# DLRM tower on one core: pairs of 8, 16, 24, six of 32 and 16 samples, layer 2 of two pairs in waits, unread products on TensorE

## The reference, cut to what matters

```python
x0 = e                       # (512, 32, 16), e[:, m] = tbl_m[ids[:, m]]
xk, outs = x0, []
for W in (W0, W1, W2):       # (32, 32, 64), (32, 64, 64), (32, 64, 64)
    xk = relu(einsum('bmd,bhd,mhk->bkd', x0, xk, W))
    outs.append(sum(xk, axis=2))
h = concatenate([concatenate(outs, 1), dense_ctx], 1)      # 512 x 208
h = maximum(h @ W_top1 + b_top1, 0)
h = maximum(h @ W_top2 + b_top2, 0)
y = h @ W_top3
```

## Time and profile before

| | |
|---|---|
| median of 3 runs | 350.59 us |
| profiled execution, its own time | 353.74 us |
| its span, first to last instruction | 351.9 us |
| TensorE matmul busy | 305.4 us (87%) |
| VectorE busy | 274.2 us (78%) |
| GpSimd busy | 254.2 us (72%) |
| ScalarE busy | 61.6 us (18%) |
| mean granted TensorE clock | 0.985 |

### The profile page before, as it was taken

The page is one execution under the profiler, slowest core; times in us unless marked ns, Lnnn a source line. Parts: engine busy times, 40 slices in busy tenths (PEclk is TensorE's granted clock), DMA queues, the critical chain, the costliest instruction groups (busy, mean ns, idle before and its releaser), DMA issues. The chain is left out here.

```text
span 351.9 us, 3914 instructions
## 1 busy us (share of the span) xinstructions
PE 305.4 (87%) x1476; PEld 112.7 (32%) x1476; DVE 274.2 (78%) x173; ACT 61.6 (18%) x122; POOL 254.2 (72%) x193
## 2 busy tenths in 40 slices
PE   0016859798999988999999999999999999998986
PEld 0013513243334222323333333233333334333426
DVE  0024949799999969999999999999999788954201
ACT  1001210301220330012201220222031104113011
POOL 5775678879788988888898879898919567917000
PEclk9999996999999999999999999999999999999998
DMA  5374956957973984286338643952580102100000
GB/s 178 45 251 83 369 111 180 376 88 213 381 149 65 279 329 80 28 337 260 56 71 303 272 72 77 378 190 61 151 327 0 45 2 63 45 2 0 0 0 0
DMA packets 52282, 52.07 MB, mean 148 GB/s; under 512 B 37574, under 2 KB 42568, under 8 KB 49064
## 3 DMA queue, kind: packets, MB, share of 16 engines
q1 hardware_dynamic: 41272, 39.92, 34.2%
q10 hardware_dynamic: 6896, 10.85, 11.5%
q0 software_dynamic: 4096, 1.06, 3.0%
HBM read 41.33 MB, written 2.10 MB: 123 GB/s over the span
## 5 line engine op out<-in xcount | busy, mean ns | idle before, releaser
L519 DVE TENSOR_TENSOR z_vector<-left,r_forms 128x2048 f32<-128x2048 f32 (+3 forms) x140 | 260.0, 1924 | 45.4 <-DMA r_forms<-x_rows 23.0
L569 PE MATMUL result<-z_vector,w_sb 128*64 128x512 f32 (+2 forms) x1056 | 213.9, 557 | 41.5 <-DVE z_vector L519 40.2
L309 POOL DMA_INDIRECT gathered_rows<-table,row_index x128 | 121.8, 951 | 41.2 <-issue 34.5
L324 POOL TENSOR_TENSOR z_pool<-r_forms,xj_forms 128x1024 f32<-128x1024 f32 (+2 forms) x60 | 131.8, 2232 | 24.7 <-PE result L569 15.0
L569 PEld LDWEIGHTS result<-z_vector,w_sb 128*64 128x64 f32 x1056 | 77.3, 142 | 172.9 <-issue 143.4
L569 PE MATMUL result<-z_pool,w_sb 128*64 128x512 f32 (+2 forms) x240 | 51.8, 571 | 0.0
L384 ACT ACTIVATE x_sb<-result 128x512 f32<-128x512 f32 (+2 forms) x27 | 14.9, 551 | 169.7 <-PE result L569 169.7
L499 DVE TENSOR_REDUCE d_sums<-x_sb 128x32 f32<-128x512 f32 (+2 forms) x27 | 16.8, 625 | 20.0 <-ACT x_sb L384 20.0
L569 PEld LDWEIGHTS result<-z_pool,w_sb 128*64 128x64 f32 x240 | 15.7, 136 | 34.1 <-issue 33.2
L368 ACT ACTIVATE left<-xj_forms 128x512 f32<-128x512 f32 (+2 forms) x36 | 18.6, 547 | 17.1 <-DMA xj_forms<-x_sb 6.8
L359 ACT ACTIVATE left<-h_form 128x512 f32<-128x512 f32 (+2 forms) x18 | 10.0, 553 | 59.8 <-DVE z_vector L519 44.9
(11 more groups left out here) (32 smaller groups left out, 28.1 us busy)
## 6 DMA issues: line engine op xcount, KB each, us to landing
r_forms<-x_rows SPq DMA_DIRECT2D x24, 1024.0 KB, 10.4
r_forms<-x_rows SPq DMA_DIRECT2D x8, 768.0 KB, 6.8
xj_forms<-x_sb ACTq DMA_DIRECT2D x24, 256.0 KB, 4.0
h_form<-x_rows SPq DMA_DIRECT2D x12, 256.0 KB, 3.0
gathered_rows<-table,row_index POOLq DMA_INDIRECT x128, 3.3
r_forms<-x_rows SPq DMA_DIRECT2D x4, 512.0 KB, 6.1
x_rows<-gathered_rows SPq DMA_DIRECT2D x24, 64.0 KB, 2.5
xj_forms<-x_sb ACTq DMA_DIRECT2D x8, 192.0 KB, 3.1
```

Of the source, the lines that this page charges most:

```text
L309: nc.gpsimd.indirect_dma_start(gathered_rows[:, half % GATHERED, g], None, table, bass.IndirectOffsetOnAxis(ap=row_index[:, at:at + 1], ax ...
L324: nc.gpsimd.tensor_tensor(z_pool[:, unit % NZP, t, :, 0:columns(p)], r_form(q, p, t)[:, s0:s1], xj1_forms[form_buffer(n, p)][:, t, 0:colum ...
L519: nc.vector.tensor_tensor(z_vector[:, unit % NV, t, 0:s1 - s0, 0:columns(p)], left[:, t, bank, 0:columns(p)].unsqueeze(1).broadcast_to([12 ...
L569: done = nc.tensor.matmul(result[n][K * t:K * t + K, 0:columns(p)], weights, z[:, t, 0:columns(p)], start=first, stop=last)
```

## The change

`SAMPLES` becomes 8, 16, 24, six of 32 and 16, so there are ten pairs in place of nine, and the first and the last are smaller. The start of the program is in another order: layer 2 of pairs 0 and 1 moves forward, between the stages of layers 0 and 1 of the next pairs, and (2, 1) is done in two parts (its units 0 and 1 before (1, 2), the others behind (0, 3)). POOL has no chunks in (1, 0), (2, 0), (1, 1) and (2, 1), 2 in (1, 2), and in the last pairs the numbers that the last pairs had before. POOL issues 12 gathers at once and 28 in fours behind waits, and then, as before, 8 behind its products of each stage in which it has chunks. TensorE gets `busy`, unread products of 256 columns, 5 and 2 and 4 and 4 of them in its waits at the start, and 3 ahead of the last part of the tower.

```diff
-SAMPLES = [16, 24] + [32] * 6 + [24]
+SAMPLES = [8, 16, 24] + [32] * 6 + [16]
...
+SPLIT = 1
+STAGES = [(0, 0, "all"), (1, 0, "all"), (0, 1, "all"), (2, 0, "all"), (1, 1, "all"), (0, 2, "all"), (2, 1, "form 0"),
+          (1, 2, "all"), (0, 3, "all"), (2, 1, "form 1")]
+for _p in range(SPLIT + 2, NP):
+    STAGES.append((1, _p, "all"))
     if _p + 1 < NP:
-        STAGES.append((0, _p + 1))
-    if _p > 0:
-        STAGES.append((2, _p - 1))
+        STAGES.append((0, _p + 1, "all"))
+    STAGES.append((2, _p - 1, "all"))
...
-GATHERS_FIRST = GATHERS_BEFORE[6]
+GATHERS_FIRST = GATHERS_BEFORE[8]
 def pool_chunks(n, p):
-    few = {(1, 0): 0, (1, 1): 2, (2, 5): 4, (2, 6): 6, (2, 7): 6, (2, 8): 4}
+    few = {(1, 0): 0, (2, 0): 0, (1, 1): 0, (2, 1): 0, (1, 2): 2, (2, 6): 4, (2, 7): 6, (2, 8): 6, (2, 9): 4}
     return few.get((n, p), 4 if n == 1 else 2)
...
@@ POOL
             gather(0, GATHERS_BEFORE[4])
-            pool.wait_ge(selected, 1)
-            for k in range(4):
-                gather(GATHERS_BEFORE[4] + 4 * k, GATHERS_BEFORE[4] + 4 * k + 4)
-                pool.wait_ge(z_vector_used, k + 2)
+            first = GATHERS_BEFORE[4]
+            pool.wait_ge(selected, selections(1, 0))
+            gather(first, first + 4)
+            pool.wait_ge(z_vector_used, VECTOR_AT[1, 0, 1] + 1)
+            gather(first + 4, first + 8)
+            pool.wait_ge(selected, selections(2, 0))
+            gather(first + 8, first + 12)
+            pool.wait_ge(z_vector_used, VECTOR_AT[0, 1, 0] + 1)
+            gather(first + 12, first + 16)
+            pool.wait_ge(selected, selections(1, 1))
+            gather(first + 16, first + 20)
+            pool.wait_ge(z_vector_used, VECTOR_AT[1, 1, 1] + 1)
+            gather(first + 20, first + 24)
+            pool.wait_ge(selected, selections(2, 1))
+            gather(first + 24, first + 28)
             first = GATHERS_FIRST
-            for n, p in STAGES:
+            for n, p in FORM1:
                 if pool_units(n, p):
                     products(n, p)
                     gather(first, first + 8)
...
@@ ACT
+            copy_xj1(1, 0)
+            copy_h(1)
+            relu(1, 0)
+            load_xj1(2, 0)
+            copy_xj1(2, 0)
+            relu(0, 1)
+            load_xj1(1, 1)
+            copy_xj1(1, 1)
+            relu(2, 0)
+            copy_h(2)
+            relu(1, 1)
+            load_xj1(2, 1)
+            relu(0, 2)
+            load_xj1(1, 2)
+            copy_xj1(1, 2)
+            copy_h(3)
+            relu(1, 2)
+            copy_xj1(2, 1)
+            relu(0, 3)
+            load_xj1(1, 3)
+            load_xj1(2, 2)
+            relu(2, 1)
+            for p in range(SPLIT + 2, NP - 1):
...
@@ DVE
             products(0, 0, 0)
+            all_products(1, 0, [(0, 0)])
+            products(0, 1, 0)
+            all_products(2, 0, [(1, 0)])
+            all_products(1, 1, [(0, 1), (2, 0)])
+            products(0, 2, 0)
+            products(2, 1, 0)
+            products(2, 1, 1)
+            all_products(1, 2, [(0, 2), (1, 1)])
+            products(0, 3, 0)
+            for k in range(2, len(vector_units(2, 1))):
+                products(2, 1, k)
+            for p in range(SPLIT + 2, NP):
...
@@ PE
+            def busy(count, bank=y_psum):
+                for _ in range(count):
+                    nc.tensor.matmul(bank[0:K, 0:4 * K], w0_sb[:, 0], w12_sb[:, 0, 0, 0:4], start=True, stop=True)
             pe.wait_ge(w0_loaded, 48)
             pe.wait_ge(w0_folded, 2)
+            pe.wait_ge(w12_loaded, 16)
+            pe.wait_ge(x0_stored[0][1], 32)
+            busy(5)
             vector_unit(0, 0, 0)
             squares(0)
             pe.wait_ge(select_loaded, 16)
             select(1, 0)
+            busy(2)
+            layer(1, 0)
+            select(2, 0)
+            busy(4)
+            vector_unit(0, 1, 0)
+            squares(1)
+            layer(2, 0, {1: [lambda: select(1, 1)]})
+            layer(1, 1)
+            select(2, 1)
+            busy(4)
+            vector_unit(0, 2, 0)
+            squares(2)
+            vector_unit(2, 1, 0)
+            vector_unit(2, 1, 1)
+            select(1, 2)
+            layer(1, 2)
...
+            busy(3, result[0])
             pe.wait_ge(late_in_ready, 6)
```

More of the change, by code:

```diff
@@ L86, in pool_units @@
     return units + [(0, s, s + 2) for s in range(4 - max(0, chunks - 4), 4, 2)]
[L89 to L96, removed]
+VECTOR_AT, POOL_BEFORE = {}, {}
+for _n, _p, _part in STAGES:
+    _count = len(vector_units(_n, _p))
+    for _k in {"all": range(_count), "form 0": range(2), "form 1": range(2, _count)}[_part]:
+        VECTOR_AT[_n, _p, _k] = len(VECTOR_AT)
+_w = 0
+for _stage in FORM1:
+    POOL_BEFORE[_stage] = _w
     _w += len(pool_units(*_stage))
@@ L106, in vector_after, with selections @@
 def vector_after(stage):
[L108 removed]
+    return VECTOR_AT[stage[0], stage[1], len(vector_units(*stage)) - 1] + 1
 def pool_after(stage):
     return POOL_BEFORE[stage] + len(pool_units(*stage))
+def selections(n, p):
+    return FORM0.index((n, p)) + 1
 def build(nc, table, ids, base, w0, w0_mirror, not_twice, w12, select, dense, w_top1, b_top1, w_top2, b_top2, w_top3,
@@ L379, in relu @@
                     if n < 2:
-                        act.wait_ge(selected, LAYER_AT[n + 1, p - 1] + 1)
+                        act.wait_ge(selected, selections(n + 1, p - 1))
                         for t in range(2):
@@ L515, in products @@
                     elif k == 0:
-                        dve.wait_ge(selected, LAYER_AT[n, p] + 1)
+                        dve.wait_ge(selected, selections(n, p))
                     if unit >= NV and t == 0:
@@ L600, in select @@
                 pe.wait_ge(x_ready[n - 1], p + 1)
-                if LAYER_AT[n, p] > 0:
-                    pe.wait_ge(z_vector_ready, 2 * (VECTOR_BEFORE[LAYERS[LAYER_AT[n, p] - 1]] + 2))
+                if selections(n, p) > 1:
+                    before = FORM0[selections(n, p) - 2]
+                    pe.wait_ge(z_vector_ready, 2 * VECTOR_AT[before[0], before[1], 1] + 2)
                 for t in range(2):
@@ L651, in _ @@
             select(1, 0)
-            pe.wait_ge(w12_loaded, 16)
-            for p in range(NP - 1):
-                layer(1, p, {1: [lambda: select(2, p - 1)]} if p > 0 else {})
+            busy(2)
[14 more added lines that the diff above has]
+            layer(1, 2)
+            vector_unit(0, 3, 0)
+            squares(3)
+            for k in range(2, len(vector_units(2, 1))):
+                vector_unit(2, 1, k, k == len(vector_units(2, 1)) - 1)
+                if k == 2:
+                    select(1, 3)
+            for p in range(SPLIT + 2, NP - 1):
+                layer(1, p, {1: [lambda: select(2, p - 1)]})
                 vector_unit(0, p + 1, 0)
                 squares(p + 1)
-                if p > 0:
-                    layer(2, p - 1, {1: [lambda: select(1, p + 1)]})
-                else:
-                    select(1, 1)
+                layer(2, p - 1, {1: [lambda: select(1, p + 1)]})
             last = NP - 1
```

57 lines of the change are left out of this document (25 added, 32 removed).

## The result

| | before | after |
|---|---|---|
| median | 351.01 us (4 runs, 350.45 to 353.13) | **419.4 us** (4 runs, 417.22 to 421.08) |
| ratio | | **1.190** [1.184, 1.196] |
| profiled execution, its own time; span | 353.74; 351.9 | 421.08; 419.3 |

The changed kernel is 19% slower. The forecast was 430 us in a range of 403 to 446.

The account below looks back on a forecast made before the run. With three engines full at once, late gathers were taken to close a loop. POOL's start 87, plus five turns of 49.4 (247), less 4.85, plus 102.5 gave span 431.7; plus 1.8, less 3.15, forecast 430 us, range 403 to 446.

Parts of the forecast that it names:

- The count of gathers: POOL's queue: 48 gathers are issued ahead of its products in (1, 3) where 56 are needed, so half 1 of pair 4 is late.
- The turn: Loop from POOL's products in (1, p) to those in (1, p+1): 49.4 us, five times from (1, 3) to (1, 8), 247 us.
- last gather to the product of half 1: SP's queue to DVE, each turn: stores, load_h and slab r0 take 16.6 us, the middle of 15.1 and 18.1.
- The half clock: TensorE in (0, p+1): after over 10 us idle, its clock falls to 1.2 GHz, adding 2.75 us a turn.
- The fill: Program start up to POOL's start in (1, 3): 87 us, bounds 83 to 91, against 78.48 before.
- The end: From the end of the squares of (0, 8) to the span's end: 102.5 us, bounds 101 to 104, against 110.3 before.
- POOL's gap: Sign on POOL: some 14 us of gap ahead of its products of (1, 4) to (1, 8), starts 49 us apart.
- VectorE's waits for r_forms: Sign on DVE: a wait of 13 to 24 us in each (0, p) from 4 to 8, the first the longest.
- idle time of TensorE: Sign on TensorE: 65 to 75 us more idle time in all, with clock 0.5 behind each wait.
- A: Rival for steady part and fill: gathers in time, fill packed, 35 us a pair, 336 us in all; chance 0.05.
- C: Rival: only the fill is worse, gathers in time; +8.5 and -7.5 us give 352 us; chance 0.03.
- B: Rival: one stall only, pair 4 late by about 14 us, then POOL catches up; 365 to 380, say 372; chance 0.06.

## Why the prediction was right, step by step

**The count of gathers.** Right, and it is the whole of the loss. 48 gathers where 56 are needed was read from the order alone; giving the eight back makes 1.190 into 0.995 on chip 2, and taking eight away makes the kernel before 434.61 us for 362.6 on chip 1.

**The turn.** Taken as 49.4 us, measured 47.2 in the mean. By its terms, for the first turn (47.1):

| term | taken | measured |
|---|---|---|
| products and gathers, 87.43 to 105.68 | 18.3 | 18.25 |
| last gather to the product of half 1, to 120.67 | 16.6 | **15.0** |
| that product, to TensorE's start at 123.01 | 2.3 | 2.3 |
| TensorE to the ReLU, to 129.88 | 7.35 | 6.9 |
| ReLU and load, to 134.49 | 4.8 | 4.6 |

The mis-sized term is the second; in the five turns it was 14.7 to 15.1 us. The two rows of before gave 15.1 and 18.1, and I took the middle. VectorE waited for the slab in both the earlier trace rows, so that does not tell them apart. From the gather to the first r0 load it is 5.8 us in both, and in the turn as well. The 3 us lie behind that: where it was 18.1, the two issues took 2.13 us for 1.24 in the turn, and the slab of half 1 landed 10.8 us after its own issue began, for 8.5. Why that one load was slower stays open, so nothing on record says beforehand which of the two values a turn would have. Over five turns the difference from 49.4 is 11 us, 8 of them from this term. Of the range's parts the quick slab with the half clock came true: 18.3 + 15.1 + 2.3 + 7.35 + 4.8 = 47.85.

**The half clock.** I took 2.75 us a turn. The matmuls of layer 0 lost 2.3, 2.6, 2.9, 3.0 and 1.4 us in the five turns (5.96 and 6.29 for 3.65 in the first two), and TensorE's busy time in the five turns is 12.0 us over that of the same work in the kernel without the loop: 2.4 a turn, 3% of the span. The unread products in the turns gave up to 2.1 us back where they held the clock. The Trainium skill ("TensorE: Matmul & The Clock Gate", "What's actually happening") advises to take the ramp as under 1% of a typical kernel's span. For one cold start the trace agrees (2.4 of 419 us, 0.6%); the five together do not, since the wait comes back in every turn. The prediction read the sentence as if it stood for all of them. By that reading the forecast would have been near 420, which is what was measured, but for another reason: the cold starts were there, and the slab was quicker.

**The fill.** POOL's start in (1, 3) was taken as 87 and came at 87.43; VectorE's start of (1, 2), at 61.26 for 60.3, with 4.8 us of wait ahead of it for 4.

**The end.** 102.5 us from the end of the squares of (0, 8); it was 419.3 - 318.5 = 100.8. Of the bounds the lower, 101, was right, but not for its reason. I tied it to the three unread products. With the gathers in time, the stretch from POOL's start in (1, 8) to the end is 95.7 to 95.8 us with the products (three traces) and 95.8 without them (two), and the last wide layer takes 2.2 us in all five.

**The sum.** 431.7 taken, 419.3 measured: 11 us from the turns, 1.7 from the end, less 0.4 in the fill.

**Signs that I named.** POOL's gap ahead of (1, 4) to (1, 7) was 13.6 to 14.4 us, as said, but 7.9 ahead of (1, 8). VectorE's waits for r_forms were 17.7, 14.6, 12.0, 12.4 and 12.5: the first is the longest, but three are just under my 13. One sign was wrong: I expected 65 to 75 us more idle time of TensorE. It is 94.3 against 46.5, so 48 more, since I forgot that its half-pace products (12 us) and the unread ones (11) count as busy.

**The rivals.** A and C need slabs that come in time; VectorE waited 12 to 18 us for the slab of each pair from 4 to 8. B needs starts that come closer again after (1, 4); the turns stayed 46 to 48 us to the end, since POOL's idle time lies ahead of products that stand in front of its gathers. What C would have been can now be seen: with the gathers in time the fill is 7.8 us longer and the end 8.4 shorter than in the kernel before with the three unread products, same chip (squares of the last pair of 32 at 246.80 for 238.97, spans 348.3 and 348.9). C said +8.5 and -7.5.

## What to carry to other kernels

When a change moves stages past each other, count for each queue what has been issued by the time it is needed, cumulatively and stage by stage; a batch that is one stage late here cost not one wait but one in every turn, because the batch behind waits for work that waits for the batch before it. The period of such a loop is the plain sum of its links, and half the lateness takes away just its share. A smaller last piece is worth what it saves only if the first pieces do not grow: here 28 or 32 samples in the second pair ate all that the last one gave.

## What the runs showed of the hardware that I had not expected

**One chip is slow at the start of the program.** On chip 1 the kernel before took 362.6 us against 352.4 on chip 2, and the kernel with the gathers back 369 to 371 against 351.5. The steady part is the same on both (turns of 33.9 us). In the fill of chip 1, TensorE's records come one by one with gaps that nothing in the profile releases:

```profile
87.79 1.50 PE L622 MATMUL result<-z_vector,w_sb 128*64 128x512 f32 x5 [1.35 <-issue]
90.46 0.59 PE L622 MATMUL result<-z_vector,w_sb 128*64 128x512 f32 x1 [1.17 <-issue]
```

where chip 2 has its records in one piece:

```profile
88.12 7.07 PE L622 MATMUL result<-z_vector,w_sb 128*64 128x512 f32 x24 [2.71 <-DVE z_vector L560]
```

The cause was not found, and no run was made to find it. It costs the kernel with more and shorter instructions in the fill more (18 to 19 us for 10), which would explain why its ratio changes sign between the chips; that is an inference, not shown.

**Of two waits, the shorter left the clock alone.** After 1.51 us without work the granted clock was still 1.00, after 3.56 us it was 0.50. The program's first products are an odd case. In the kernel before, the first 16 records of 256 columns took as long as 32 of them do later in the earlier trace rows, while the granted clock reads 1.00 from 23 to 28 us:

```profile
25.01 3.68 PE L569 MATMUL result<-z_vector,w_sb 128*64 128x256 f32 x16 [25.01 <-DVE z_vector L519]
```

So in this trace the column does not show the slow start, and the lengths of the records do.

With its gathers in time the changed kernel is 0.5% [0.2, 0.8] faster than the kernel before on chip 2, and 2% slower on chip 1.
